# Relative-position attention between two feed-forward layers: query rows in two kinds with both halves, and head 0 staged from small transfers of the last batch

## The chip, the cores and the metric

The kernel runs on one core of a Trainium2 chip. A core has TensorE (PE, matrix products; its weight loads are listed as PEld), VectorE (DVE), ScalarE (ACT), GpSimd (POOL) and SyncE (SP), each with its own instruction stream, and 16 DMA engines that move data for all of them. Streams meet only at semaphores. The metric is the device time of one execution: before the change the median of three runs is 445.53 us (445.25 to 446.58).

## The reference

Input x is 4 batches of 512 tokens with 128 features, in float32. Three steps follow each other, each added to x:

```
x = x + 0.5 * ffn(layernorm(x))
x = x + attention(layernorm(x))          # 16 heads of width 8, with relative positions
x = x + 0.5 * ffn(layernorm(x))
ffn(x):   layernorm, product with ternary w1 (512 x 128), gelu, layernorm, product with ternary w2
attention(x):
  content = (q + u) k^T ;  pos = relative_shift((q + v) P^T),  P = sinusoids @ Wp + bp
  out = softmax((content + pos) / sqrt(8)) v ;  return out @ Wo + bo
```

The relative shift makes row s of the positional scores up to column s from query s, and the columns from s + 2 on from query s + 1.

## The kernel before, in words

The program has three stretches: the first feed-forward with the projections of attention at its end, the 16 heads, and the output projection with the second feed-forward. `ffn` is a software pipeline written out by hand: each engine's stream runs through the same steps n = 0 to 26, and `QK_STEPS` says that the query and key products of batch 0, 1, 2, 3 stand at steps 17, 20, 22, 24. The value products (`v_product`, L1066, in 16 groups) stand between and behind them.

Scores are made in float16 at float32 precision by splitting queries, keys and positions into a high and a low half. PE makes a projection, ACT writes the high halves (`q_high_halves`, L566; `k_high_half`, L574), DVE the low halves (`q_low_halves`, L854; `k_low_half`, L866, for batch 3), and POOL extends the positional query by the first 64 entries of the next position (L481, L482) and makes the low keys of batches 0 to 2 (L486). `uh, ul` are the halves of q + u, `vh, vl` those of q + v, `kh, kl` those of the key.

The products of one head need these values with other rows on the partitions than the projections leave them on. So all of them go through scratch in device memory: SP writes each batch for all 16 heads at once (the loop at L340, seven transfers of 256 KB a batch: three of queries to `qs_scratch`, two of content rows to `qc_scratch`, two of keys to `kc_scratch`), and each head is then loaded into `stage_q`, `stage_c`, `stage_k` and `stage_z`, which have two halves each (`par`), so that one head is loaded while another is computed. For head 0, POOL loads the content rows of all batches and two of the eight pieces of `stage_q`, and SP the other six (L362) and the keys (L364), once `q_out` and `k_out` say that every write has landed.

A head has 16 score tiles q of 128 rows (four column groups j of PE with 32 rows each: 4 batches by 8 positions; the query position is 128 j + 8 q + i). One tile (`scores`, L1102) is four rounds over the four column groups: the content product (L1116, 512 columns), the low query half against the high positions (L1122, 512 columns), the high query half against both position halves for the columns up to the diagonal (L1128, a0 + 8 columns, a0 = 128 j + 8 q) and the next query's high half for those behind it (L1133, 510 - a0 columns). Two tiles make a pair in a PSUM pair (three PSUM pairs take turns). For each pair DVE takes the row maxima (`row_max`, L886), ACT the exponentials (L633), DVE turns them (`turn`, L894), and PE multiplies them with the values (`values`, L1139), one head later. Heads 0, 1, 2 and 15 are written out; heads 3 to 14 are a loop of six rounds of two heads on each engine.

Before head 0 PE waits for the copies of all values, for the folded output bias (L1097 on PE, L876 on DVE, semaphore `bo_ready`) and for head 0's loads.

## Time and profile before

| | |
|---|---|
| median of three runs | 445.53 us |
| the profiled execution's own time | 447.46 us |
| its span, first to last instruction | 445.3 us |
| busy: DVE, PE, ACT, POOL | 398.2 us (89%), 357.0 us (80%), 263.9 us (59%), 113.4 us (25%) |
| DMA queues | 30.67 MB, mean 69 GB/s |

The times in the rows below count from the first instruction, so the time outside the span (447.46 - 445.3 = 2.16 us) lies around them. A busy share is an average over the three stretches. The chain of waits is followed back from the last instruction; at each step it names what released it. "issue" in a bracket is idle time of an engine for which the profile shows no wait.

### The profile page before, as it was taken

To read this page: it belongs to the slowest core of one execution; us is meant where nothing else is said; L and a number is where in the kernel's file an instruction comes from. 1 tells how busy PE (TensorE), PEld (TensorE's weight loads), DVE (VectorE), ACT (ScalarE), POOL (GpSimd) and SP (SyncE) were. 2 spreads that over 40 slices of the span, in tenths; PEclk is the share of its full clock that TensorE was granted. 3 is DMA by queue.
4 is the path that set the end of the run, shared out by engine and by line. 5 is a ranking of instruction groups with operands and counts; after the bars stand their busy time and mean duration, and the time that the engine had idled before them with its cause. 6 is when DMAs were issued, how large, how long until landed. Compare 5 with 4: busy or idle time off the path is not lost.

```text
span 445.3 us, 18049 instructions
## 1 busy us (share of the span) xinstructions
PE 357.0 (80%) x7328; PEld 288.1 (65%) x7328; DVE 398.2 (89%) x579; ACT 263.9 (59%) x650; POOL 113.4 (25%) x157
## 2 busy tenths in 40 slices
PE   1869898756979889898898987988989889676974
PEld 1647675645767767677676766776767767573664
DVE  8786988429999999999999999999999999948685
ACT  1666555316666666666666666666666666614980
POOL 7543745390020201202102022020120210025552
PEclk9988899969899999999999999999999999988898
DMA  7005147920322313213133132231321301500002
GB/s 213 1 1 186 51 148 245 296 62 12 81 57 43 81 26 87 68 31 84 40 65 75 19 88 56 44 80 20 88 64 30 89 7 25 75 18 2 0 26 71
DMA packets 60182, 30.67 MB, mean 69 GB/s; under 512 B 36880, under 2 KB 58928, under 8 KB 60016
## 3 DMA queue, kind: packets, MB, share of 16 engines
q1 hardware_dynamic: 59376, 29.22, 25.8%
q10 hardware_dynamic: 576, 0.73, 0.6%
q8 instruction: 27, 0.44, 0.4%
q0 software_dynamic: 192, 0.18, 0.2%
q14 instruction: 11, 0.09, 0.1%
HBM read 19.11 MB, written 11.01 MB: 68 GB/s over the span
## 4 chain that ended last, share of the span: by engine, by line
DVE 58%; issue 17%; PE 11%; ACT 5%; POOL 2%; SPq 2%; DMA 2%; DVEq 1%; POOLq 0%; ACTq 0%
DVE pT L894 30%; DVE negmax L886 19%; PE pair L1014 3%; ACT v_rep L602 2%; DVE xh L702 2%; ACT v_rep L590 1%; PE pair L969 1%; DVE v_rep L820 1%; DVE sqsum L814 1%; DMA qs_scratch<-pT 1%; SPq L309 1%; PE pair L1183 1%; DMA stage_k<-kc_scratch 1%; DVE stat L692 1%; PE pair L1116 1%
## 5 line engine op out<-in xcount | busy, mean ns | idle before, releaser
L633 ACT ACTIVATE probs<-pair,negmax 128x512 f32<-128x512 f32 x256 | 173.7, 683 | 111.3 <-DVE negmax L886 111.3
L886 DVE TENSOR_REDUCE negmax<-pair 128x2 f32<-128x1024 f32 x128 | 152.1, 1188 | 10.4 <-PE pair L1133 10.4
L894 DVE STREAM_TRANSPOSE pT<-probs 128x1024 f32<-128x1024 f32 x128 | 157.0, 1226 | 0.5 <-ACT probs L633 0.5
L1116 PE MATMUL pair<-stage_k,stage_c 128*32 128x512 f16 x1024 | 117.2, 408 | 47.4 <-ACT probs L633 40.8
L1122 PE MATMUL pair<-stage_z,stage_q 128*32 128x512 f16 x1024 | 111.4, 384 | 0.0
L1133 PE MATMUL pair<-stage_z,stage_q 128*32 128x438 f16 (+58 forms) x1024 | 102.9, 282 | 0.0
L508 POOL COPY v_diag<-v_rep 32x512 f32 (+1 forms) x64 | 38.9, 607 | 233.9 <-PE pair L1148 226.5
L1128 PE MATMUL pair<-stage_z,stage_q 128*32 128x16 f16 (+50 forms) x1024 | 97.9, 277 | 0.0
L1148 PE MATMUL pair<-pT,v_diag 128*32 128x128 f32 (+1 forms) x2176 | 93.3, 271 | 3.6 <-DVE pT L894 3.6
L1116 PEld LDWEIGHTS pair<-stage_k,stage_c 128*32 128x32 f16 x1024 | 50.7, 140 | 69.5 <-ACT probs L633 55.4
L1148 PEld LDWEIGHTS pair<-pT,v_diag 128*32 128x32 f32 x2176 | 73.3, 114 | 4.1 <-DVE pT L894 3.8
L1133 PEld LDWEIGHTS pair<-stage_z,stage_q 128*32 128x32 f16 x1024 | 47.8, 136 | 11.9 <-issue 1.2
L1128 PEld LDWEIGHTS pair<-stage_z,stage_q 128*32 128x32 f16 x1024 | 47.7, 135 | 11.9 <-issue 1.6
L1122 PEld LDWEIGHTS pair<-stage_z,stage_q 128*32 128x32 f16 x1024 | 50.2, 147 | 0.0
L633 ACT ACTIVATION_READ_ACCUMULATOR probs<-pair,negmax (+1 forms) x256 | 50.1, 196 | 0.0
L1014 PEld LDWEIGHTS pair<-w2c,v_rep 128*128 128x128 f32 x256 | 35.7, 211 | 3.6 <-issue 1.5
L1014 PE MATMUL pair<-w2c,v_rep 128*128 128x129 f32 x256 | 36.9, 297 | 0.0
L590 ACT ACTIVATE v_rep<-pair,vectors,cols 128x512 f32<-128x512 f32 x32 | 25.0, 780 | 11.7 <-PE pair L1014 7.2
L602 ACT ACTIVATE v_rep<-v_rep,cols 128x512 f32<-128x512 f32 x32 | 23.2, 725 | 1.2 <-DVE sqsum L814 1.2
L814 DVE TENSOR_TENSOR sqsum<-sqsum,v_rep 128x512 f32<-128x512 f32 x16 | 14.2, 884 | 6.3 <-ACT v_rep L602 5.5
L702 DVE TENSOR_SCALAR xh<-x,mv,rs 128x128 f32<-128x128 f32 x48 | 16.7, 410 | 3.2 <-POOL rs L440 3.2
L969 PE MATMUL pair<-ident,xh 128*128 128x128 f32 x48 | 12.8, 357 | 7.5 <-DVE xh L702 7.5
(112 smaller groups left out, 326.0 us busy)
## 6 DMA issues: line engine op xcount, KB each, us to landing
stage_z<-z_scratch SPq DMA_DIRECT2D x16, 254.0 KB
qs_scratch<-pT SPq DMA_DIRECT2D x12, 256.0 KB, 2.7
stage_q<-qs_scratch SPq DMA_DIRECT2D x126, 24.0 KB
stage_z<-z_scratch SPq DMA_DIRECT2D x16, 128.0 KB
qc_scratch<-pT SPq DMA_DIRECT2D x8, 256.0 KB, 3.5
kc_scratch<-pT SPq DMA_DIRECT2D x8, 256.0 KB, 3.5
stage_k<-kc_scratch SPq DMA_DIRECT2D x16, 128.0 KB
stage_z<-z_scratch SPq DMA_DIRECT2D x16, 127.5 KB
```

The source lines that it names most:

```text
L508: nc.gpsimd.tensor_copy(v_diag[q, par, :, quad, :], v_rep[q, :, bass.ds(h * HP, HP)]).then_inc(v_diag_ready, 1)
L590: nc.scalar.activation(ge[:, n % 8, :], ps[n % 2], ACT.Gelu, scale=wstep[:, 0:1], bias=b1c[:, c:c + 1]).then_inc(s["gelu"], 1)
L602: nc.scalar.activation(sq[:, m % 3, :], ge[:, m % 8, :], ACT.Square, bias=minus_pivot).then_inc(s["squared"], 1)
L633: nc.scalar.activation(probs[:, q % 6, :], score_pair(q // 2)[:, q % 2, :], ACT.Exp, bias=negmax[:, q % 8:q % 8 + 1], accum_out=rowsum[:, ...
L886: nc.vector.tensor_reduce(negmax[:, 2 * n % 8:2 * n % 8 + 2], score_pair(n)[:, :, :], AX.X, ALU.max, negate=True).then_inc(max_ready, 1)
L894: nc.vector.transpose(pT[:, par, 2 * n:2 * n + 2, :].rearrange("p a s -> p (a s)"), probs[:, 2 * n % 6:2 * n % 6 + 2, :].rearrange("p a s ...
L1014: ins = mm(out_tile(t), ge[:, (4 * g + c) % 8, k], w2c[:, c, :], start=(c == 0), stop=(c == HC - 1))
L1116: mm(bank[32 * j:32 * j + 32, :], all_rows[:, 32 * j:32 * j + 32], stage_k[:, par, :], start=True, stop=False, skip_group_check=True)
L1122: mm(o, rows(stage_q[:, par, 0, :], j), stage_z[:, par, 0, m0:m0 + S], start=False, stop=False, skip_group_check=True)
L1128: mm(bank[32 * j:32 * j + 32, 0:n], rows(stage_q[:, par, 1, :], j), stage_z[:, par, 1, m0:m0 + n], start=False, stop=False, skip_group_che ...
L1133: ins = mm(bank[32 * j:32 * j + 32, a0 + 2:S], rows(stage_q[:, par, 2, :], j), stage_z[:, par, 2, m0 + a0 + 2:m0 + S], start=False, stop=True,
L1148: ins = mm(ps[4 + par][32 * b:32 * b + 32, NI * q0:NI * q1], v_diag[:, par, b * KB + kb, :, :].rearrange("p j e -> p (j e)"), mov, start=( ...
```

## The change

Positional queries have two kinds instead of three: one for this position and one for the next, each with the low and the high half as rows. The positions have a low and a high version of either part. One tile is five rounds over the column groups: the content product, and then, for each position half, a0 + 8 columns with this query and 510 - a0 columns with the next. The queries of a batch are one write of 288 KB instead of three of 256 KB, and a piece of `stage_q` is 64 runs of 256 bytes instead of 192 of 128. The scratch for content and keys is laid out by head.

Head 0's keys come straight from on-chip memory (`first_keys`): POOL sends those of batches 0 to 2 behind their low halves, SP those of batch 3. The writes of batch 3 are split: what head 0 needs (the queries of its 8 features in both kinds come from 16 partitions, content from 8) goes out first; SP then sends four query pieces and the last content rows of head 0, waits until all eleven loads of its own have landed, and only then writes the keys of batch 2 and everything else of batch 3. POOL loads the other four query pieces of head 0, and, between the two spreads of the values, the eight of head 1. The halves move to another part of `pT`, and DVE's wait for all writes goes from before head 0 to the first turn of head 1; one of DVE's clears of `stage_q` at the start goes, and POOL's one.

```diff
@@ -50,18 +50,22 @@
-LOADS_FIRST = 6
-LOADS = 16
+LOADS_EVEN = 11
+LOADS_ODD = 9
+LOADS_POOL = 13
+EARLY = 2 * HP
+LOADS = 17
+ZR = ZW - ZB0
...
-    qs_dram = nc.dram_tensor("qs_scratch", (D, 2, 3, B * S), F16, kind="Internal").ap()
-    qc_dram = nc.dram_tensor("qc_scratch", (D, 4, B * S), F16, kind="Internal").ap()
-    kc_dram = nc.dram_tensor("kc_scratch", (D, 4, B, S), F16, kind="Internal").ap()
-    z_dram = nc.dram_tensor("z_scratch", (D, 2, 3, 2 * S), F16, kind="Internal").ap()
+    qs_dram = nc.dram_tensor("qs_scratch", (D, 2, B, VW), F16, kind="Internal").ap()
+    qc_dram = nc.dram_tensor("qc_scratch", (H, B, 2, HP, 2, S), F16, kind="Internal").ap()
+    kc_dram = nc.dram_tensor("kc_scratch", (H, B, 2, HP, 2, S), F16, kind="Internal").ap()
+    z_dram = nc.dram_tensor("z_scratch", (D, 2, 4, 2 * S), F16, kind="Internal").ap()
...
-        stage_q = sb("stage_q", [128, 2, 3, B * S], F16)
+        stage_q = sb("stage_q", [128, 2, B * NI, 2, NG], F16)
...
-        stage_z = sb("stage_z", [128, 2, 3, ZW], F16)
+        stage_z = sb("stage_z", [128, 2, 2, S + ZR], F16)
...
+        def first_keys(eng, b, done):
+
+            c = slice(b * S, (b + 1) * S)
+            for a in range(2):
+                r = 32 * b + 16 * a
+                eng.dma_start(stage_k[r:r + 16, 0, :], rep_ap(half[0:HP, 2 + a, c], [(0, 2), (1, S)]))\
+                    .then_inc(done, 16)
 
         def stage_queries(eng, h, par, done, rows_i=range(NI)):
-            q_rows = qs_dram.rearrange("(h p) t k n -> h (p t) k n", p=HP)[h]
+            q_rows = qs_dram.rearrange("(h p) t b n -> h (p t) b n", p=HP)[h]
             for ii in rows_i:
                 i = NI - 1 - ii
-                src = q_rows.rearrange("r k (b m) -> r (k b) m", b=B)[:, :, i * NG:(i + 1) * NG]
-                dst = stage_q[16 * ii:16 * ii + 16, par, :, :].rearrange(
-                    "r k (b m) -> r (k b) m", b=B)[:, :, i * NG:(i + 1) * NG]
-                eng.dma_start(dst, src).then_inc(done, 16)
+                dst = stage_q[16 * ii:16 * ii + 16, par, :, :, :].rearrange("r (b i) k g -> r b i (k g)", b=B)[:, :, i]
+                eng.dma_start(dst, q_rows[:, :, i * NG:(i + 2) * NG]).then_inc(done, 16)
+
+        def write_queries(eng, b, r, done):
+
+            eng.dma_start(qs_dram[r, :, b, :], rep_ap(vl[r, b, :], [(VQ, 2), (1, VW)])).then_inc(done, 16)
+
+        def write_content(eng, b, h0, h1, done):
+            c = slice(b * S, (b + 1) * S)
+            for a in range(2):
+                eng.dma_start(qc_dram[h0:h1, b, a].rearrange("h p d n -> h (p d n)"), half[HP * h0:HP * h1, 0:2, c])\
+                    .then_inc(done, 16)
+
+        def write_keys(eng, b):
+            c = slice(b * S, (b + 1) * S)
+            for a in range(2):
+                eng.dma_start(kc_dram[:, b, a].rearrange("h p d n -> h (p d n)"),
+                              rep_ap(half[:, 2 + a, c], [(0, 2), (1, S)])).then_inc(k_out, 16)
...
-            for b in range(B):
-                c = slice(b * S, (b + 1) * S)
-
-                sp.wait_ge(q_split, 2 * b + 1)
-                sp.dma_start(qs_dram[:, :, 1, c], rep_ap(vh[:, b, :], [(0, 2), (1, S)])).then_inc(q_out, 16)
+            for b in range(B - 1):
+
                 sp.wait_ge(v_extended, 2 * b + 2)
-                sp.dma_start(qs_dram[:, :, 0, c], rep_ap(vl[:, b, :], [(NG, 2), (1, S)])).then_inc(q_out, 16)
-                sp.dma_start(qs_dram[:, :, 2, c], rep_ap(vh[:, b, NG:], [(0, 2), (1, S)])).then_inc(q_out, 16)
-
+                write_queries(sp, b, slice(0, D), q_out)
                 sp.wait_ge(q_split, 2 * b + 2)
-                for t, src in ((0, uh), (2, ul)):
-                    sp.dma_start(qc_dram[:, t:t + 2, c], rep_ap(src[:, c], [(0, 2), (1, S)]))\
-                        .then_inc(u_out[b], 16)
-                if b < B - 1:
+                write_content(sp, b, 0, H, u_out[b])
+                if b < B - 2:
                     sp.wait_ge(k_split, b + 1)
-                else:
-                    sp.wait_ge(k_split_last, 1)
-                for t in (0, 2):
-                    sp.dma_start(kc_dram[:, t:t + 2, b, :], rep_ap(kh[:, c], [(B * S, 2), (1, S)]))\
-                        .then_inc(k_out, 16)
-            sp.wait_ge(q_out, 16 * 3 * B)
-            sp.wait_ge(stage_zero, 8)
-            stage_queries(sp, 0, 0, staged[0], range(NI - 2))
-            sp.wait_ge(k_out, 32 * B)
-            stage_keys(sp, 0, 0, staged[0])
+                    write_keys(sp, b)
+            sp.wait_ge(v_extended, 2 * B)
+            write_queries(sp, B - 1, slice(0, EARLY), q_first)
+            sp.wait_ge(q_split, 2 * B)
+            write_content(sp, B - 1, 0, 1, u_first)
+            sp.wait_ge(k_split_last, 1)
+            first_keys(sp, B - 1, staged[0])
+            sp.wait_ge(q_out, 16 * (B - 1))
+            sp.wait_ge(q_first, 16)
+            sp.wait_ge(stage_zero, 6)
+            stage_queries(sp, 0, 0, staged[0], range(4))
+            sp.wait_ge(u_first, 32)
+            stage_content(sp, 0, 0, B - 1, staged[0])
+
+            sp.wait_ge(staged[0], 16 * LOADS_EVEN)
+            sp.wait_ge(k_split, B - 1)
+            write_keys(sp, B - 2)
+            write_queries(sp, B - 1, slice(EARLY, D), q_out)
+            write_content(sp, B - 1, 1, H, u_out[B - 1])
+            write_keys(sp, B - 1)
 
             for b in range(B):
                 sp.wait_ge(u_out[b], 32)
                 stage_content(sp, 1, 1, b, staged[1])
+            sp.wait_ge(k_out, 32 * B)
             stage_keys(sp, 1, 1, staged[1])
-            stage_queries(sp, 1, 1, staged[1])
...
-            nc.gpsimd.memset(stage_q[:, 1, 2, :].bitcast(U32), 0).then_inc(stage_zero, 1)
...
+                        if b < B - 1:
+                            pool.wait_ge(k_split, b + 1)
+                            first_keys(pool, b, staged_pool)
...
+                        stage_content(pool, 0, 0, b, staged_pool)
...
-            pool.wait_ge(q_out, 16 * 3 * B)
-            pool.wait_ge(stage_zero, 8)
-            stage_queries(pool, 0, 0, staged_first, range(NI - 2, NI))
-            pool.wait_ge(u_out[B - 1], 32)
-            stage_content(pool, 0, 0, B - 1, staged_first)
+            pool.wait_ge(stage_zero, 6)
+            pool.wait_ge(q_out, 16 * (B - 1))
+            pool.wait_ge(q_first, 16)
+            stage_queries(pool, 0, 0, staged_pool, range(4, NI))
...
             spread_v(0, 0)
+            pool.wait_ge(q_out, 16 * B)
+            stage_queries(pool, 1, 1, staged_second)
             spread_v(1, 1)
...
+                    act.wait_ge(z_out, 16 * 2)
...
-            for par, n in ((0, 0), (0, 1), (0, 2), (1, 0), (1, 1)):
-                nc.vector.memset(stage_q[:, par, n, :].bitcast(U32), 0).then_inc(stage_zero, 1)
+            for par in range(2):
+                for b in (0, 2):
+                    nc.vector.memset(stage_q[:, par, b * NI:(b + 2) * NI, :, :].bitcast(U32), 0)\
+                        .then_inc(stage_zero, 1)
...
-            for b in range(B):
-                dve.wait_ge(u_out[b], 32)
-            dve.wait_ge(k_out, 32 * B)
-            dve.wait_ge(q_out, 16 * 3 * B)
...
+                if n == 0 and isinstance(h, int) and h == 1:
+
+                    for b in range(B):
+                        dve.wait_ge(u_out[b], 32)
+                    dve.wait_ge(k_out, 32 * B)
+                    dve.wait_ge(q_out, 16 * B)
...
-                for j in range(4):
-                    a0 = 128 * j + NI * q
-                    o = bank[32 * j:32 * j + 32, :]
-                    m0 = S - NI - a0
-                    mm(o, rows(stage_q[:, par, 0, :], j), stage_z[:, par, 0, m0:m0 + S], start=False,
-                       stop=False, skip_group_check=True)
-                for j in range(4):
-                    a0 = 128 * j + NI * q
-                    n = a0 + NI
-                    m0 = S - NI - a0
-                    mm(bank[32 * j:32 * j + 32, 0:n], rows(stage_q[:, par, 1, :], j),
-                       stage_z[:, par, 1, m0:m0 + n], start=False, stop=False, skip_group_check=True)
-                for j in range(4):
-                    a0 = 128 * j + NI * q
-                    m0 = S - NI - a0
-                    ins = mm(bank[32 * j:32 * j + 32, a0 + 2:S], rows(stage_q[:, par, 2, :], j),
-                             stage_z[:, par, 2, m0 + a0 + 2:m0 + S], start=False, stop=True,
-                             skip_group_check=True)
+
+                for low in range(2):
+                    for j in range(4):
+                        a0 = 128 * j + NI * q
+                        n = a0 + NI
+                        m0 = S - NI - a0
+                        mm(bank[32 * j:32 * j + 32, 0:n], stage_q[:, par, :, 0, j * NQ + q],
+                           stage_z[:, par, low, m0:m0 + n], start=False, stop=False, skip_group_check=True)
+                    for j in range(4):
+                        a0 = 128 * j + NI * q
+                        n = S - a0 - 2
+                        ins = mm(bank[32 * j:32 * j + 32, a0 + 2:S], stage_q[:, par, :, 1, j * NQ + q],
+                                 stage_z[:, par, low, S:S + n], start=False, stop=low == 1, skip_group_check=True)
...
-            pe.wait_ge(staged_first, 16 * LOADS_FIRST)
-            head(0, 0, 16 * (LOADS - LOADS_FIRST), True)
-            head(1, 1, 16 * LOADS)
-            head(2, 0, 16 * (2 * LOADS - LOADS_FIRST))
+            pe.wait_ge(staged_pool, 16 * LOADS_POOL)
+            head(0, 0, 16 * LOADS_EVEN, True)
+            pe.wait_ge(staged_second, 16 * NI)
+            head(1, 1, 16 * LOADS_ODD)
```

The order on SP, from the end of batch 2 to the loads of head 1. Before, batch 2 and 3 are written whole, then head 0's queries and keys are loaded, then head 1:

```order
L344 DMA qs_scratch<-pT 256x1x512
L346 DMA qs_scratch<-pT 256x1x512
L347 DMA qs_scratch<-pT 256x1x512
L351 DMA qc_scratch<-pT 128x2x512 x2
L358 DMA kc_scratch<-pT 128x2x512 x2
L309 DMA stage_q<-qs_scratch 16x12x64 x6
L300 DMA stage_k<-kc_scratch 128x1x512
L296 DMA stage_c<-qc_scratch 32x4x128 x4
L300 DMA stage_k<-kc_scratch 128x1x512
L309 DMA stage_q<-qs_scratch 16x12x64 x8
```

On SP now, from the queries of batch 2:

```order
L325 DMA qs_scratch<-pT 256x1x576
L330 DMA qc_scratch<-pT 16x16x512 x2
L325 DMA qs_scratch<-pT 32x1x576
L330 DMA qc_scratch<-pT 16x1x512 x2
L313 DMA stage_k<-pT 16x1x512 x2
L321 DMA stage_q<-qs_scratch 16x4x128 x4
L303 DMA stage_c<-qc_scratch 32x4x128
L336 DMA kc_scratch<-pT 16x16x512 x2
L325 DMA qs_scratch<-pT 224x1x576
L330 DMA qc_scratch<-pT 15x16x512 x2
L336 DMA kc_scratch<-pT 16x16x512 x2
L303 DMA stage_c<-qc_scratch 32x4x128 x4
```

Between the end of the projections and head 0's last load, five small transfers stand on SP where seven of 256 KB stood, and the large ones stand behind head 0's loads.

The order on POOL, from the keys of batch 2 to the values' spread (`stage_c` are content rows, `v_diag` the values in the layout of the product). Before:

```order
L486 TENSOR_TENSOR pT<-pT 128x512
L296 DMA stage_c<-qc_scratch 32x4x128
L481 COPY pT<-pT 128x64
L482 COPY pT<-pT 128x64
L296 DMA stage_c<-qc_scratch 32x4x128
L309 DMA stage_q<-qs_scratch 16x12x64 x2
L296 DMA stage_c<-qc_scratch 32x4x128
L511 MEMSET v_diag 128x2048
L508 COPY v_diag<-v_rep 32x64x8 x8
```

On POOL now:

```order
L517 TENSOR_TENSOR pT<-pT 128x512
L313 DMA stage_k<-pT 16x1x512 x2
L303 DMA stage_c<-qc_scratch 32x4x128
L512 COPY pT<-pT 128x64
L513 COPY pT<-pT 128x64
L303 DMA stage_c<-qc_scratch 32x4x128
L321 DMA stage_q<-qs_scratch 16x4x128 x4
L544 MEMSET v_diag 128x2048
L541 COPY v_diag<-v_rep 32x64x8 x4
L321 DMA stage_q<-qs_scratch 16x4x128 x8
L541 COPY v_diag<-v_rep 32x64x8 x4
```

Two key transfers stand ahead of batch 3's extension, and head 1's queries are POOL's, between the two spreads.

The order on PE in the first tile of head 0. Before, four rounds of four (the two rounds of 512 columns are each one row):

```order
L1116 MATMUL pair<-stage_k,stage_c 32x512 x4
L1122 MATMUL pair<-stage_z,stage_q 32x512 x4
L1128 MATMUL pair<-stage_z,stage_q 32x8
L1128 MATMUL pair<-stage_z,stage_q 32x136
L1128 MATMUL pair<-stage_z,stage_q 32x264
L1128 MATMUL pair<-stage_z,stage_q 32x392
L1133 MATMUL pair<-stage_z,stage_q 32x510
L1133 MATMUL pair<-stage_z,stage_q 32x382
L1133 MATMUL pair<-stage_z,stage_q 32x254
L1133 MATMUL pair<-stage_z,stage_q 32x126
```

On PE now, the same tile up to the second half's first four products; the other four follow as in the first half:

```order
L1150 MATMUL pair<-stage_k,stage_c 32x512 x4
L1158 MATMUL pair<-stage_z,stage_q 32x8
L1158 MATMUL pair<-stage_z,stage_q 32x136
L1158 MATMUL pair<-stage_z,stage_q 32x264
L1158 MATMUL pair<-stage_z,stage_q 32x392
L1163 MATMUL pair<-stage_z,stage_q 32x510
L1163 MATMUL pair<-stage_z,stage_q 32x382
L1163 MATMUL pair<-stage_z,stage_q 32x254
L1163 MATMUL pair<-stage_z,stage_q 32x126
L1158 MATMUL pair<-stage_z,stage_q 32x8
L1158 MATMUL pair<-stage_z,stage_q 32x136
L1158 MATMUL pair<-stage_z,stage_q 32x264
```

A tile has 20 products instead of 16, and a column group streams 512 + 2 x 518 = 1548 columns instead of 2 x 512 + 518 = 1542.

## Rows read from the trace of the kernel before

**Rows 1.** Chain of waits, projections to head 0: start us, us, what.

```profile
73.93 0.76 DVE pT L862
...
81.22 4.43 DMA qs_scratch<-pT
...
89.84 3.66 DMA stage_k<-kc_scratch
...
93.64 0.65 PE pair L1116 x4
...
98.77 1.23 DVE negmax L886
```

**Rows 2.** Timeline, 76 to 97.5 us: start, us, engine, what, [idle before <-releaser].

```profile
77.71 0.24 POOL L482 COPY pT<-pT 128x64 f16<-128x64 f16 x1
78.43 0.74 DVE L869 SCALAR_TENSOR_TENSOR pT<-pair,vectors,pT 128x512 f16<-128x512 f32 x1
...
85.67 4.13 SPq L309 DMA_DIRECT2D stage_q<-qs_scratch  x6
...
86.78 0.55 POOL L309 DMA_DIRECT2D stage_q<-qs_scratch  x1 [0.29 <-issue]
87.28 0.28 DVE L876 TENSOR_TENSOR rows<-rows,pair 128x128 f32<-128x128 f32 x1
...
89.78 5.28 POOL L508 COPY v_diag<-v_rep 32x512 f32<-32x512 f32 x8
...
96.61 1.23 DVE L886 TENSOR_REDUCE negmax<-pair 128x2 f32<-128x1024 f32 x1 [9.05 <-PE pair L1133]
```

**Rows 3.** Busy time by stretch: us, engines' busy (instructions), granted clock, DMA share, GB/s.

```profile
79.40:83.20 3.80, 3.70 (x128) 3.49 (x128) 1.75 (x3) 1.07 (x2) 0.55 (x1) 1.00 1.03 341
83.20:84.30 1.10, 0.01 (x1) 0.00 (x2) 0.00 (x0) 0.12 (x1) 0.00 (x0) 1.00 0.82 254
...
93.60:97.80 4.20, 4.16 (x52) 2.66 (x56) 1.19 (x1) 0.00 (x0) 4.00 (x6) 0.50 0.31 66
```

**Rows 4.** Issue to landing of the `qs_scratch` transfers, 68 to 100 us.

```profile
DMA to landing us min/median/max: 2.4/2.7/4.4
```

**Rows 5.** Issue to landing of the 64 KB `attn_scratch` transfers.

```profile
DMA to landing us min/median/max: 2.0/2.1/3.8
```

**Rows 6.** Timeline of PE, 108.5 to 119 us: head 1's first product.

```profile
112.25 0.66 PE L1116 MATMUL pair<-stage_k,stage_c 128*32 128x512 f16 x4 [3.02 <-ACT probs L633]
```

**Rows 7.** Timeline, start of the program.

```profile
4.63 0.95 POOL L427 MEMSET stage_q<- 128x1024 uint32 x1
...
5.32 0.91 DVE L718 MEMSET stage_q<- 128x1024 uint32 x1 [0.16 <-issue]
...
6.14 0.81 DVE L692 BATCH_NORM_STATS2 stat<-x 128x6 f32<-128x128 f32 x4
```

**Rows 8.** Issue to landing of the transfers of x (0.7 to 2.3 us).

```profile
DMA to landing us min/median/max: 4.7/6.4/7.8
```

**Rows 9.** Timeline, one tile in the loop of heads.

```profile
174.89 0.40 PE L1122 MATMUL pair<-stage_z,stage_q 128*32 128x512 f16 x4
...
175.10 0.37 PE L1128 MATMUL pair<-stage_z,stage_q 128*32 128x208 f16 x4
...
175.32 0.42 PE L1148 MATMUL pair<-pT,v_diag 128*32 128x128 f32 x8
```

**Rows 10.** Busy time of one head in the loop.

```profile
148.95:167.01 18.06, 15.54 (x388) 12.70 (x392) 18.06 (x17) 11.74 (x34) 2.42 (x5) 1.00 0.28 63
```

**Rows 11.** Timeline, 184.5 to 189 us: the loop's jump back.

```profile
185.03 0.44 PE L1116 MATMUL pair<-stage_k,stage_c 128*32 128x512 f16 x4 [1.18 <-ACT probs L633]
...
187.40 1.19 DVE L886 TENSOR_REDUCE negmax<-pair 128x2 f32<-128x1024 f32 x1
```

**Rows 12.** The page's DMA queues: packets, MB, share of 16 engines.

```profile
q8 instruction: 27, 0.44, 0.4%
```

**Rows 13.** DMA queues from 200 to 260 us.

```profile
DMA packets 9510, 3.74 MB, mean 62 GB/s; under 512 B 7206, under 2 KB 9510, under 8 KB 9510
...
q1 hardware_dynamic: 9510, 3.74, 26.5%
```

More of the change, by code:

```diff
@@ L117, in macaron_kernel @@
         pf = pTf[:, 3584:4096]
-        half = pTf[:, 4096:8192].bitcast(F16).rearrange("p (a n) -> p a n", a=4)
+        half = pTf[:, 10240:14336].bitcast(F16).rearrange("p (a n) -> p a n", a=4)
         uh, ul, kh, kl = (half[:, n, :] for n in range(4))
+        VQ = 2 * (14336 - 8192)
         vl = pTf[:, 8192:8192 + B * VW // 2].bitcast(F16).rearrange("p (b n) -> p b n", b=B)
@@ L206, in macaron_kernel @@
         staged = [sem("staged_even"), sem("staged_odd")]
-        staged_first = sem("staged_first")
+        q_first = sem("q_first")
+        u_first = sem("u_first")
+        staged_pool = sem("staged_pool")
+        staged_second = sem("staged_second")
         v_diag_ready = sem("v_diag_ready")
@@ L325, in _ @@
             sp.wait_ge(pos_split, 2)
-            for t, kind, src in ((0, 0, 0), (1, 0, 2), (0, 1, 0), (1, 1, 1), (0, 2, 2), (1, 2, 3)):
-                sp.dma_start(z_dram[:, t, kind, :], zs[:, src, :]).then_inc(z_out, 16)
+            for t in range(2):
+                sp.dma_start(z_dram[:, t, :, :], zs).then_inc(z_out, 16)
             def stage_pos(h, par):
                 z_rows = z_dram.rearrange("(h p) t k n -> h (p t) k n", p=HP)[h]
-                for kind, lo, hi in ((0, 0, ZW), (1, 0, S), (2, ZB0, ZW)):
-                    zr = z_rows[:, kind, :]
-                    src = bass.AP(zr.tensor, zr.offset + lo, [[1, NI]] + [list(zr.ap[0])] + [[1, hi - lo]])
-                    sp.dma_start(stage_z[:, par, kind, lo:hi], src).then_inc(staged[par], 16)
@@ L336, in _ @@
[L336 removed]
+                for low in range(2):
+                    for kind, lo, at, n in ((low, 0, 0, S), (2 + low, ZB0, S, ZR)):
+                        zr = z_rows[:, kind, :]
+                        src = bass.AP(zr.tensor, zr.offset + lo, [[1, NI]] + [list(zr.ap[0])] + [[1, n]])
+                        sp.dma_start(stage_z[:, par, low, at:at + n], src).then_inc(staged[par], 16)
+            sp.wait_ge(z_out, 16 * 2)
             stage_pos(0, 0)
             stage_pos(1, 1)
[L340 to L344 removed]
+            for b in range(B - 1):
@@ L1107, in scores @@
                 bank = score_pair(q // 2)[:, q % 2, :]
-                def rows(a, j):
-                    return a.rearrange("k (b g) -> k b g", g=NG)[:, :, j * NQ + q]
                 all_rows = stage_c[:, par, :].rearrange("k (m g) -> k m g", g=NQ)[:, :, q]
@@ L1164, in head @@
                         values(h - 1, 1 - par, kb)
-            pe.wait_ge(staged_first, 16 * LOADS_FIRST)
-            head(0, 0, 16 * (LOADS - LOADS_FIRST), True)
-            head(1, 1, 16 * LOADS)
-            head(2, 0, 16 * (2 * LOADS - LOADS_FIRST))
+            pe.wait_ge(staged_pool, 16 * LOADS_POOL)
+            head(0, 0, 16 * LOADS_EVEN, True)
+            pe.wait_ge(staged_second, 16 * NI)
+            head(1, 1, 16 * LOADS_ODD)
+            head(2, 0, 16 * (LOADS + LOADS_EVEN))
             with pe.Fori(0, (H - 4) // 2) as it:
                 for k in range(2):
-                    head(it * 2 + (3 + k), 1 - k, (it + (2 + k)) * (16 * LOADS) - 16 * LOADS_FIRST * k)
-            head(H - 1, 1, (H // 2) * 16 * LOADS)
+                    head(it * 2 + (3 + k), 1 - k,
+                         (it + (1 + k)) * (16 * LOADS) + 16 * (LOADS_EVEN if k else LOADS_ODD))
+            head(H - 1, 1, 16 * ((H // 2 - 1) * LOADS + LOADS_ODD))
             for kb in range(KB):
```

11 lines of the change are left out of this document (4 added, 7 removed).

## The prediction

> **What bounds the kernel now.** Start with the busy time of one head in the loop: in 18.06 us DVE is busy for all 18.06 and PE for 15.54 [rows 10]. From its second row maximum on, DVE sets the pace of the heads, and PE waits for banks. So an edit of the products is worth something only where PE runs out of those 2.5 us, and an edit of the transfers only where DVE waits. Next read the chain of waits: between the projections (DVE, 73.93) and the second row maximum of head 0 (98.77) it runs over a landing of `qs_scratch`, a landing of `stage_k`, and PE at 93.64 [rows 1]. The timeline says the same from DVE's side: its first row maximum starts at 96.61 after 9.05 us idle, though the last projection half was made at 78.43 + 0.74 = 79.17 [rows 2]. In between, the DMA share is 1.0 at 341 GB/s [rows 3]: SP's large writes fill the DMA engines, and the loads of head 0 stand behind them. When PE gets its data it is at half clock (0.50 of full, 1.2 GHz) after the idle time [rows 3]. This stretch is what the change edits.
>
> **The change part by part.**
>
> *Head 0's loads.* All of this is worked out from rows of one execution, which took 447.46 us; the savings are taken off the median, 445.53, which is 1.93 below it.
> The last extension ends at 77.71 + 0.24 = 77.95 [rows 2]. Ahead of it POOL now issues two key transfers, 0.55 each as its other issues [rows 2]; part of that 1.1 falls into a wait for DVE, and I take 78.6 (77.95 to 79.05). SP was still issuing for batch 2 then; now it has three transfers in that batch instead of seven and is free. It issues five small transfers and then four query pieces and a content row. Its pitch in the loads of before is 4.13 / 6 = 0.69 [rows 2], so the loads begin at 78.6 + 5 x 0.69 = 82.05 and the fifth is issued at 84.8. The first transfer's landing (2.1 by the 64 KB transfers, 3.8 at most [rows 5]) is at 80.7 to 82.4, hidden behind the issues up to 3.45. The last load lands 2.7 later (2.4 to 4.4, [rows 4]): 87.5, bounds 87.2 to 89.2. POOL's four pieces start after that first landing and its content row at about 81.3; with 0.55 + 0.29 a piece [rows 2] the last is issued at 83.8 and lands at 86.5.
> What would be late next is the bias on DVE, 87.28 + 0.28 = 87.56 [rows 2], at the end of the value products. These lose 1.10 us between 83.20 and 84.30, with PE and PEld idle, right behind a stretch of exactly 128 products (256 instructions with their weight loads) at DMA share 1.03 [rows 3]. I read that as PE waiting for its next block of instructions behind the writes, since 27 transfers of 0.44 MB in all are 16 KB each [rows 12]. With fewer writes the stall may go, and then this gate is at 86.5. So PE starts head 0 at 87.6 (86.5 to 89.4) instead of 93.64.
>
> *The clock.* PE is then idle for about 1 us between the value products and head 0. After 1.18 us idle it took 0.44 for a 512-column product [rows 11], after the long wait 0.65 [rows 1]; I take full clock. A tile's last three rounds take 0.43 [rows 9] and the first, of 512 columns like the second, 0.22: 0.65 in all. Two pairs are 2.6 us, so the second row maximum, the step at which DVE's pace sets in, starts at 87.6 + 2.6 + 0.1 = 90.3 instead of 98.77: 8.5 saved. Bounds: with PE at 86.5 9.6 saved; with PE at 89.4 and at half clock, 98.77 - 93.64 = 5.13 for the two pairs as before [rows 1], 94.5, 4.3 saved.
>
> *The held-back writes.* They are 512 + 252 + 480 + 512 = 1756 KB, at 341 GB/s [rows 3] 5.3 us, begun at 87.5 and landed by 95 with 2.1 for the last. Behind them SP issues head 1's content rows and keys: seven writes and five loads at 0.69 end at 95.8, landed by 100.2 at the slow bound. On POOL the first four copies of the values (half of 5.28 [rows 2]) end near 91; the queries have landed near 92 (third of SP's writes); eight pieces at 0.84 are issued until 97.8 and landed at 100.5 (102.2 at 4.4). The spread of head 1's values waits behind them, but it is used a head later. Head 1 started 112.25 - 98.77 = 13.5 after the second row maximum [rows 1, 6], released by a bank and not by its loads; that is 103.8 now. So the writes are hidden with 1.6 to 3.6 us to spare. They do load the DMA engines while PE fetches head 0's products: one stall as at 83.20, up to 1.10. PE is one pair ahead of DVE then, so I take 0.3 (0 to 1.1).
>
> *The start.* DVE's clears are 0.91 with 0.16 between [rows 7]; one less lets its first statistics start 1.07 earlier, at 5.07, but x needs 0.7 + 4.7 = 5.4 to land [rows 7, 8]. POOL loses 0.95 [rows 7]. So up to 0.7 is gained at the head of a chain that continues into the feed-forward; part goes into PE's slow start. I take 0.4 (0 to 0.7).
>
> *The products.* In the loop, round 2 starts at 174.89, round 3 at 175.10 and the next work behind round 4 at 175.32 [rows 9]: rounds 3 and 4 together cost 0.22, as round 2 does (0.21), since the short and the long columns add up to 518 in each column group. Replacing round 2 by another round 3 and 4 costs 0.01 a tile, 0.2 a head. Were each added round of four to cost a further 0.1, it would be 1.6 a head, still inside PE's 2.5. DVE hides it: 0. Positions, layout of the scratch and the longer runs of `stage_q` are loads one head ahead: 0.
>
> Sum: -8.5 - 0.4 + 0.3 = -8.6, so 445.53 - 8.6 = 436.9.
>
> **The rivals.**
>
> *Late loads.* Two transfers in a row at their slow bounds (3.8 and 4.4), or SP's issue of odd shapes slower than 0.69. For it: the chain has two landings in series, and issues have taken longer while the engines were full. Against: the writes ahead are small and the engines nearly empty by then. PE starts at 89.4, cold, and DVE at 94.5: -4.3 - 0.4 + 0.3, 441.1. If POOL's issues slow down beside DVE, head 1 is late by a few us instead; same price.
>
> *The loop of heads outgrows PE's instruction store.* This is the one on the other side. A head in the loop has 256 + 128 = 384 products (x388 counted [rows 10]) and as many weight loads; two heads are 1536 instructions, 6 blocks of 256. From 200 to 260 us all 9510 packets are those of the data queue [rows 13], so before the change PE jumps back five times without fetching anything. Now two heads are 2 x 448 x 2 = 1792 instructions, 7 blocks. If they no longer fit, with edges and the block fetched ahead, each jump waits for a block. Under full DMA engines a block took 3.8 + 1.1 = 4.9 us [rows 3]; a small transfer lands in 2.1 [rows 5]. Hidden at the jump are 1.18 of idle PE and the 187.40 - (185.03 + 1.6) = 0.8 by which the first pair is early [rows 11], 2.0 in all. Five jumps cost 5 x 0.1 = 0.5 to 5 x 2.9 = 14.5. It outweighs the gain when a block takes over 2.0 + 8.6 / 5 = 3.7 us; at 4.9 the time is 451.4. Half way, at 3.3, it is 443.4. For it: 7 is more than any loop in this trace. Against: the fetches may be short at the DMA share of 0.28 in the loop [rows 10].
> The Trainium skill, in "Runtime: NRT & Kernel Launch" under "Instruction fetch mechanics", gives PE 128 KiB of instruction memory, 2048 instructions in 16 KiB blocks, and says that a taken branch whose target is not in the current two-page window must fetch the target before going on. The trace disagrees on the window: a loop of 6 blocks was not fetched again [rows 13]; with 8 blocks in all, 7 blocks that start inside one, and one ahead, would be 9, and the sum would be the rival's.
>
> *The stretch is bound by something else.* If the value products and the bias keep their place and clock, PE cannot start before 87.6 anyway; that is in the forecast. No row speaks for a gate later than that.
>
> **How the numbers follow.** The forecast, 436.9, has a chance of 0.56, with its own range 435 to 439.5. Late loads (or a late head 1): 0.22. The loop fetching again: 0.20, of which 0.07 below 441, 0.05 between 441 and 446.9, 0.08 beyond. Others 0.02. The range 434.8 to 443 leaves out some 0.15. A difference of under 0.3%, 1.3 us, cannot be told from none: faster means below 444.2, slower above 446.9. From the cases: faster 0.85, same 0.06, slower 0.09.
>
> **What would show it.** Right: no 1.1 us hole in the value products; PE's first product of head 0 near 87.6 at clock 1.0; the second row maximum near 90; head 1's first product released by ACT; a head of 18.06 us in the loop with PE busy about 15.8; instruction transfers of the page up from 27 to about 30 only (six written heads or loop bodies by 128 more instructions are 3 blocks), none inside the loop. Wrong: DVE idle in the loop right behind a jump, with instruction packets there; PE released by `stage_q` or `stage_c` after 89; head 1 released by a landing; DVE busy under 18.0 of each 18.06.

## The result, and the profile after

The kernel after takes 454.17 us (median of four runs, 451.56 to 457.29) against 445.43 for the kernel before beside it (445.25 to 446.58): a ratio of 1.018, 95% interval 1.014 to 1.022. It is slower by 8.7 us; the forecast was 436.9 with a range to 443.0. The profiled execution took 454.7 us, with a span of 452.6 (before: 447.46 and 445.3).

Head 0 starts as early as forecast, and earlier. The chain of waits of the kernel after, from the projections to the first row maximum (start us, us, what), answers to [rows 1]:

```profile
70.49 0.76 DVE pT L900
...
78.98 0.65 SPq L321
...
81.60 2.83 DMA stage_c<-qc_scratch
...
84.56 0.41 PE pair L1150 x2
...
86.33 1.24 DVE negmax L919
```

The timeline of the same stretch (start, us, engine, what, [idle before <-releaser]) answers to [rows 2]:

```profile
74.95 0.24 POOL L513 COPY pT<-pT 128x64 f16<-128x64 f16 x1
...
76.66 3.70 PE L1122 MATMUL pair<-pT,xT 128*32 128x128 f32 x128 [0.79 <-issue]
...
80.67 2.34 PE L1122 MATMUL pair<-pT,xT 128*32 128x128 f32 x74 [0.31 <-issue]
...
83.66 0.28 DVE L914 TENSOR_TENSOR rows<-rows,pair 128x128 f32<-128x128 f32 x1
...
84.56 0.44 PE L1150 MATMUL pair<-stage_k,stage_c 128*32 128x512 f16 x4 [1.13 <-DMA stage_c<-qc_scratch]
...
87.81 1.23 DVE L919 TENSOR_REDUCE negmax<-pair 128x2 f32<-128x1024 f32 x1 [0.26 <-PE pair L1163]
```

The second row maximum, from which DVE sets the pace, starts at 87.81 instead of 98.77 [rows 1]: 10.96 us earlier. 3.44 of that came before the change's stretch (the chain's first row at 70.49 instead of 73.93), 7.5 in it. The busy time by stretch (us, PE, PEld, DVE, ACT, POOL busy with their instructions, granted clock with 1.00 for TensorE's full speed, DMA share, GB/s) has the projections' end without the full DMA engines of [rows 3], head 0's first products at full clock, a head in the loop, and the first 4 us behind one of the loop's jumps:

```profile
75.00:84.00 9.00, 7.33 (x235) 6.46 (x226) 4.29 (x8) 3.60 (x5) 4.62 (x9) 1.00 0.35 80
84.50:88.00 3.50, 3.44 (x99) 3.37 (x102) 1.42 (x2) 0.41 (x1) 1.89 (x4) 1.00 0.65 179
...
148.95:167.01 18.06, 16.07 (x452) 14.05 (x448) 18.06 (x17) 11.66 (x34) 2.43 (x4) 1.00 0.23 56
...
176.00:180.00 4.00, 3.13 (x48) 2.52 (x52) 0.83 (x2) 1.09 (x4) 0.32 (x1) 0.57 0.36 96
```

So a head still takes 18.06 us with DVE busy throughout, as in [rows 10]; PE's part rose from 15.54 to 16.07. The last row shows where the time went: DVE busy for 0.83 of 4 us. All five jumps look like that in the timeline. PE's first product of a round and DVE's first row maximum of it stand below, and last PE's first product behind the loop, where nothing jumps back; [rows 11] has the same place of before:

```profile
173.39 0.69 ACT L669 ACTIVATE probs<-pair,negmax 128x512 f32<-128x512 f32 x1 [0.81 <-DVE negmax L919]
...
176.87 0.66 PE L1150 MATMUL pair<-stage_k,stage_c 128*32 128x512 f16 x4 [3.72 <-ACT probs L669]
...
179.83 1.22 DVE L919 TENSOR_REDUCE negmax<-pair 128x2 f32<-128x1024 f32 x1 [3.17 <-PE pair L1163]
...
216.09 0.44 PE L1150 MATMUL pair<-stage_k,stage_c 128*32 128x512 f16 x4 [3.54 <-ACT probs L669]
217.88 1.23 DVE L919 TENSOR_REDUCE negmax<-pair 128x2 f32<-128x1024 f32 x1 [1.81 <-PE pair L1163]
...
255.13 0.66 PE L1150 MATMUL pair<-stage_k,stage_c 128*32 128x512 f16 x4 [4.54 <-ACT probs L669]
258.09 1.23 DVE L919 TENSOR_REDUCE negmax<-pair 128x2 f32<-128x1024 f32 x1 [3.98 <-PE pair L1163]
...
295.12 0.44 PE L1150 MATMUL pair<-stage_k,stage_c 128*32 128x512 f16 x4 [4.31 <-ACT probs L669]
297.39 1.22 DVE L919 TENSOR_REDUCE negmax<-pair 128x2 f32<-128x1024 f32 x1 [3.07 <-PE pair L1163]
...
334.23 0.66 PE L1150 MATMUL pair<-stage_k,stage_c 128*32 128x512 f16 x4 [3.93 <-ACT probs L669]
337.19 1.23 DVE L919 TENSOR_REDUCE negmax<-pair 128x2 f32<-128x1024 f32 x1 [3.36 <-PE pair L1163]
...
371.07 0.44 PE L1150 MATMUL pair<-stage_k,stage_c 128*32 128x512 f16 x4 [1.16 <-ACT probs L669]
```

The brackets name ACT, because its exponential was the last semaphore that PE needed. It is not the cause: the exponential that frees the first bank ended at 173.39 + 0.69 = 174.08, and PE started 2.8 us later. Before, PE began 1.18 us after its last work [rows 11]; behind the loop it still does (1.16). What PE waited for shows in the times of the instruction transfers: in each round the first one behind the jump starts 1.3 to 2.7 us after the jump, and PE's first weight load comes 2.7 to 3.2 us after that start. Three of the five restarts are at half clock (0.66 for a 512-column product instead of 0.44); a fourth, at 295.12, begins at full clock and falls to half within its first pair (0.52 from 296.0 to 298.0 us).

DVE's waits in the heads, 110 to 385 us (line waited for: us in total, times, longest):

```profile
DVE negmax L919 <- PE pair L1163: 15.4, 5, 4.0
```

The page's DMA queues (packets, MB, share of 16 engines) have more instruction transfers than [rows 12]; at 1.23 MB for 75 they too are 16 KB each:

```profile
q8 instruction: 75, 1.23, 1.2%
```

and the queues from 200 to 260 us, where [rows 13] had none, now show them inside the loop:

```profile
q1 hardware_dynamic: 6800, 3.19, 20.6%
q8 instruction: 14, 0.23, 1.7%
```

The account, profiled run against profiled run: second row maximum -10.96; from there to the last turn 391.94 - 87.81 = 304.13 instead of 386.56 - 98.77 = 287.79, +16.34, of which the five waits are 15.4; behind it +1.92. Together +7.3, the difference of the spans. Of the 1.92, 1.63 stand at the tail's 32 turns on PE (L1214), which took 5.47 us here and 3.84 before; in the written-out kernel below they take 3.84 again.

### The profile page after: what moved, and what is told of

The parts are those of the page before. It is cut to its first block, busy times and chain, and to the rows that moved or that the text cites. A ratio compares the mean times of both kernels' runs of the same rounds, so it can differ in the third digit from the quotient of the medians.

```text
span 452.6 us, 20122 instructions
## 1 busy us (share of the span) xinstructions
PE 367.0 (81%) x8352; PEld 313.5 (69%) x8352; DVE 398.4 (88%) x578; ACT 263.8 (58%) x650; POOL 120.3 (27%) x171
## 3 DMA queue, kind: packets, MB, share of 16 engines
q8 instruction: 75, 1.23, 1.2%
## 4 chain that ended last, share of the span: by engine, by line
DVE 57%; issue 17%; PE 12%; ACT 7%; POOL 3%; SPq 1%; DVEq 1%; DMA 1%; POOLq 0%; ACTq 0%
DVE pT L933 29%; DVE negmax L919 19%; PE pair L1053 3%; ACT v_rep L638 2%; PE pair L1163 2%; PE pair L1150 2%; DVE xh L738 2%; ACT v_rep L626 1%; PE pair L1008 1%; PE pair L1214 1%; ACT probs L669 1%; DVE v_rep L858 1%; DVE sqsum L852 1%; PE pair L1158 1%; ACT xT L598 1%
## 5 line engine op out<-in xcount | busy, mean ns | idle before, releaser
L1163 PE MATMUL pair<-stage_z,stage_q 128*32 128x510 f16 (+34 forms) x2048 | 181.7, 287 | 0.0
L1158 PE MATMUL pair<-stage_z,stage_q 128*32 128x8 f16 (+34 forms) x2048 | 170.5, 283 | 0.0
L1150 PE MATMUL pair<-stage_k,stage_c 128*32 128x512 f16 x1024 | 134.5, 409 | 44.3 <-ACT probs L669 40.5
L919 DVE TENSOR_REDUCE negmax<-pair 128x2 f32<-128x1024 f32 x128 | 152.2, 1189 | 18.6 <-PE pair L1163 18.5
L1158 PEld LDWEIGHTS pair<-stage_z,stage_q 128*32 128x32 f16 x2048 | 135.6, 142 | 0.4
L1163 PEld LDWEIGHTS pair<-stage_z,stage_q 128*32 128x32 f16 x2048 | 112.8, 138 | 11.1 <-issue 2.3
L1177 PE MATMUL pair<-pT,v_diag 128*32 128x128 f32 (+1 forms) x2176 | 103.4, 268 | 3.5 <-DVE pT L933 3.5
L1150 PEld LDWEIGHTS pair<-stage_k,stage_c 128*32 128x32 f16 x1024 | 60.9, 142 | 62.6 <-ACT probs L669 55.3
L1053 PEld LDWEIGHTS pair<-w2c,v_rep 128*128 128x128 f32 x256 | 34.6, 205 | 3.5 <-issue 1.4
L1053 PE MATMUL pair<-w2c,v_rep 128*128 128x129 f32 x256 | 35.7, 291 | 0.0
L1008 PEld LDWEIGHTS pair<-ident,xh 128*128 128x128 f32 x48 | 7.4, 160 | 13.9 <-DVE xh L738 10.9
L1122 PE MATMUL pair<-pT,xT 128*32 128x128 f32 x512 | 15.4, 274 | 1.8 <-issue 1.1
```

The source lines that it names most:

```text
L919: nc.vector.tensor_reduce(negmax[:, 2 * n % 8:2 * n % 8 + 2], score_pair(n)[:, :, :], AX.X, ALU.max, negate=True).then_inc(max_ready, 1)
L1053: ins = mm(out_tile(t), ge[:, (4 * g + c) % 8, k], w2c[:, c, :], start=(c == 0), stop=(c == HC - 1))
L1150: mm(bank[32 * j:32 * j + 32, :], all_rows[:, 32 * j:32 * j + 32], stage_k[:, par, :], start=True, stop=False, skip_group_check=True)
L1158: mm(bank[32 * j:32 * j + 32, 0:n], stage_q[:, par, :, 0, j * NQ + q], stage_z[:, par, low, m0:m0 + n], start=False, stop=False, skip_grou ...
L1163: ins = mm(bank[32 * j:32 * j + 32, a0 + 2:S], stage_q[:, par, :, 1, j * NQ + q], stage_z[:, par, low, S:S + n], start=False, stop=low == ...
L1177: ins = mm(ps[4 + par][32 * b:32 * b + 32, NI * q0:NI * q1], v_diag[:, par, b * KB + kb, :, :].rearrange("p j e -> p (j e)"), mov, start=( ...
```

## The experiments

Two theories went in. *The store*: PE's loop body, 1818 instructions with its waits and branch instead of 1562, no longer stays in PE's instruction memory, so each jump waits for it to be fetched. *The work*: five rounds of products instead of four use up PE's spare time at the place where the heads change, and PE comes late by itself.

**The loop written out on PE alone**, in the kernel after (no jump is left; same products):

```diff
-            with pe.Fori(0, (H - 4) // 2) as it:
+            for it in range((H - 4) // 2):
                 for k in range(2):
                     head(it * 2 + (3 + k), 1 - k,
```

> The changed kernel with PE's loop over heads 3 to 14 written out, so that PE never jumps back; nothing else differs. Theory S (store): a loop of two heads of 896 instructions no longer stays in PE's instruction store, and each of five jumps waits for a block; DVE's five waits of together 15.4 us in the changed kernel go, and the time falls from 454.2 to about 439 (437 to 441), with instruction fetches spread evenly over the heads. Theory W (work): PE is late at a head's end because of 64 more products and weight loads a head; the time stays within 451 to 457.

Measured: 437.39 us (436.80 to 438.97) against 446.01 for before in that batch; ratio 0.979 (0.973 to 0.985). DVE's waits from 110 to 385 us are gone but for one of another kind:

```profile
DVE pT L933 <- ACT probs L669: 0.5, 1, 0.5
```

The page counts 65 instruction transfers here too, since straight code has to be fetched once as a whole:

```profile
q8 instruction: 65, 1.06, 1.0%
```

So neither the work nor the number of transfers costs time in the heads; what costs is waiting for them behind a jump. This kernel beats both others.

**The same edit in the kernel before.**

> The kernel before with PE's loop written out. Theory S: its loop of 6 blocks was kept, so its five jumps cost nothing and writing it out gives nothing: 445.4, within 1.3 us. If jumps cost something whatever the size of the loop, it gets faster by what five jumps cost (over 3 us).

Measured: 446.06 (445.26 to 447.25) against 446.01, ratio 0.998 (0.995 to 1.001). Before the change the jumps cost nothing, so the gain above is not one that writing out gives by itself.

**The kernel before with a body as long as after's.** Four products of one column more in each tile, which write where the content product then writes:

```diff
                 bank = score_pair(q // 2)[:, q % 2, :]
 
+                for j in range(4):
+                    mm(bank[32 * j:32 * j + 32, 0:1], stage_c[:, par, 0:32], stage_k[:, par, 0:1],
+                       start=True, stop=True, skip_group_check=True)
```

> The kernel before with four one-column products ahead of each tile (their result is overwritten by the tile's first round). PE's program is then as long as the changed one's, instruction for instruction in number (1818 from loop start to jump, at the same place), but transfers, queries and columns are those of before. Theory S: the five stalls come back, 445.4 + 15.4 = 461 (455 to 464), with some 75 instruction transfers on the page instead of 27. Theory W: four products of one column cost at most 0.1 us a tile, which PE's 2.5 idle us a head hide: 445 to 447.

Measured: 464.55 (463.27 to 467.65) against 446.01, ratio 1.040 (1.032 to 1.048). The page and DVE's waits (110 to 390 us):

```profile
q8 instruction: 75, 1.23, 1.1%
```

```profile
DVE negmax L886 <- PE pair L1136: 18.4, 9, 4.6
```

That is 0.55 above the range expected. The 18.5 us that it lost are about these 18.4 (before has one such wait, of 0.4). Five of the nine waits stand behind the five jumps (2.1 to 4.6 each), the others are under 0.6. Nothing of the change is in this kernel but the length.

**The kernel after with a loop of three rounds of four heads**, two jumps instead of five:

```diff
-            with pe.Fori(0, (H - 4) // 2) as it:
-                for k in range(2):
+            with pe.Fori(0, (H - 4) // 4) as it:
+                for k in range(4):
...
```

> The changed kernel with four heads in PE's loop and three rounds instead of two heads and six rounds: two jumps instead of five. Theory S: three stalls fewer, 454.2 - 3 x 3.1 = 445 (442 to 448). Theory W: no change, 451 to 457.

Measured: 445.01 (444.01 to 447.60) against 446.01, ratio 0.998 (0.994 to 1.001). DVE's waits, two of them behind jumps (3.9 each):

```profile
DVE negmax L919 <- PE pair L1163: 8.1, 3, 3.9
```

Five, two and no jumps give 454.2, 445.0 and 437.4: 3.4 to 3.8 us a jump. Each of the two jumps is followed by 16 instruction transfers, for a body of 3634 instructions, where the five have 9 each, and costs about the same: PE waits for the code at the jump, and the rest comes while it works. The store holds; the work falls.

**The written-out kernel again, as the base of the next two.**

> The kernel after with the loop of heads written out on PE, again, as the base of the next three runs. It should repeat 437.4 (436.8 to 439.0).

Measured: 438.88 (438.59 to 439.39) against 446.13, ratio 0.983 (0.978 to 0.988). It repeats within 1.5 us. The trace shows a difference at head 0: PE's first product takes 0.44 here too, but then the clock falls (0.55 from 86.5 to 90.3 us), and the second row maximum starts at 90.37 instead of 88.04 in the first run.

**The clears of before at the start**: the fifth on DVE and POOL's ahead of its first layer norm.

```diff
+            nc.gpsimd.memset(stage_q[:, 1, 2 * NI:4 * NI, :, :].bitcast(U32), 0).then_inc(stage_zero, 1)
             nc.gpsimd.memset(v_diag[:, 0, :, :, :], 0.0).then_inc(v_diag_zero, 1)
...
-            for par in range(2):
-                for b in (0, 2):
-                    nc.vector.memset(stage_q[:, par, b * NI:(b + 2) * NI, :, :].bitcast(U32), 0)\
-                        .then_inc(stage_zero, 1)
+            for n in (0, 2):
+                nc.vector.memset(probs[:, n:n + 2, :].bitcast(U32), 0)
+            for par, b in ((0, 0), (0, 2), (1, 0)):
+                nc.vector.memset(stage_q[:, par, b * NI:(b + 2) * NI, :, :].bitcast(U32), 0).then_inc(stage_zero, 1)
```

> The kernel after with PE's heads written out, and at the start the number of clears of before: five on DVE and one of POOL's ahead of its first layer norm (two of DVE's five clear a buffer that nothing reads until it is rewritten). If the fewer clears are worth what DVE's first normalised tile shows, 8.76 to 7.87 or 8.33, this run takes 0.4 to 0.9 more than its base: 437.8 to 438.3, and the first row maximum of head 0 moves by as much. Rival: the earlier start changes the clock or the overlap inside the first feed-forward and so is worth the whole 3.4 by which its last step came earlier in the profiled run; then this run takes 440.5 to 441.

Measured: 439.56 (438.37 to 439.73), 0.7 above its base, with ranges that overlap. So the start is not worth 3.4; what it is worth is not settled. In the two profiled runs the clears make DVE's first normalised tile 0.62 us later (8.76 for 8.14), but the last step of the projections only 0.07 (75.70 for 75.63). The first row maximum moved by 1.61 (89.40 for 87.79), more than expected, and that came behind the projections: SP's first small write is issued 0.39 later and PE's first product is at half clock (0.65).

**Without holding back**: SP sends the 1756 KB right ahead of head 0's pieces.

```diff
             first_keys(sp, B - 1, staged[0])
+            sp.wait_ge(k_split, B - 1)
+            write_keys(sp, B - 2)
             sp.wait_ge(q_out, 16 * (B - 1))
+            write_queries(sp, B - 1, slice(EARLY, D), q_out)
+            write_content(sp, B - 1, 1, H, u_out[B - 1])
+            write_keys(sp, B - 1)
             sp.wait_ge(q_first, 16)
...
-            sp.wait_ge(staged[0], 16 * LOADS_EVEN)
-            sp.wait_ge(k_split, B - 1)
-            write_keys(sp, B - 2)
-            write_queries(sp, B - 1, slice(EARLY, D), q_out)
-            write_content(sp, B - 1, 1, H, u_out[B - 1])
-            write_keys(sp, B - 1)
```

> The kernel after with PE's heads written out, where SP sends the keys of batch 2 and the large writes of batch 3 (1756 KB) right ahead of head 0's four query pieces and content row, instead of behind their landing; head 0's small writes and its keys from on-chip memory stay as they are. If holding back is what makes head 0 early, the writes cost their own time in the DMA engines, 1756 KB at 341 GB/s = 5.1 us, and seven issues at 0.7 us on SP ahead of the loads, 4.9 us: the first row maximum goes from 86.5 to some 91.5 and the time to 442.5 (441 to 444). Rival: the small writes and direct keys alone give the gain, since the loads share the engines with the writes: SP's issues still cost some, and the time is 437.5 to 439.5.

Measured: 444.65 (443.61 to 447.42) against 438.88 for the base: 5.8 lost, a little more than expected, and the first row maximum is at 93.56 instead of some 91.5. The timeline shows how:

```profile
79.71 1.28 SPq L336 DMA_DIRECT2D kc_scratch<-pT  x2
...
85.42 2.81 SPq L321 DMA_DIRECT2D stage_q<-qs_scratch  x4
...
90.63 0.65 PE L1149 MATMUL pair<-stage_k,stage_c 128*32 128x512 f16 x4 [8.55 <-DMA stage_c<-qc_scratch]
...
93.56 1.23 DVE L918 TENSOR_REDUCE negmax<-pair 128x2 f32<-128x1024 f32 x1 [10.98 <-PE pair L1162]
```

SP issues the writes for 85.42 - 79.71 = 5.7 us before it comes to the loads, and PE then starts at half clock. With the writes sent first, the rest of the change gives 446.13 - 444.65 = 1.5 us.

**Where the store ends.** The padding of above with two and with three products a tile, in bodies of 1690 and 1754 instructions:

> The kernel before with two more products of one column in every score tile (they write where the content product then writes, so the result is the same): PE's loop of heads has 1690 instructions, between the 1562 of before, which were not fetched again, and the 1818 of after, which were. If what counts is the whole of some 2048 instructions with a block of 256 fetched ahead, the loop touches 8 blocks and is fetched again each round: 65 to 75 instruction transfers, DVE waits of 3 to 4 us behind each of five jumps, 457 to 463. Rival: a loop below 7 blocks (1792) stays: 27 to 30 transfers, no such waits, 446 to 447 (two short products a tile are 0.1 us each at most, inside PE's spare time).

Measured: 445.98 (444.67 to 446.32) against 446.13, ratio 0.998 (0.995 to 1.001), and on the page

```profile
q8 instruction: 29, 0.48, 0.4%
```

That is the second expectation; the first fails. The body of 1690 stays, with no instruction transfer between its jumps, and two short products a tile cost nothing.

> The kernel before with three more products of one column in every score tile: PE's loop has 1754 instructions. 1690 were kept and 1818 fetched again. If seven whole blocks of 256 (1792) can be kept, this one stays: 27 to 30 instruction transfers, no waits behind the jumps, 446 to 447. Rival: the block fetched ahead and the loop's unaligned ends count too and the limit lies between 1690 and 1754: 65 to 75 transfers, DVE waits of 3 to 4 us at five jumps, 457 to 463.

Measured: 469.23 (467.94 to 470.52) against 448.18 for before in that batch, ratio 1.048 (1.034 to 1.062); page and DVE's waits (110 to 390 us):

```profile
q8 instruction: 75, 1.23, 1.1%
```

```profile
DVE negmax L886 <- PE pair L1136: 23.7, 9, 5.3
```

64 instructions more a body turn a kernel as fast as before into one that is 21 us slower, more than the rival expected: the five waits behind the jumps are 3.5 to 5.3. The limit lies between 1690 and 1754 here. The padding also moves the body's start (by 96 instructions from the one to the other), so whether its length or its place against the blocks decides is open. The traces speak for the place: in the first round 6 instruction transfers start while the body of 1690 runs, as with the 1562 of before, and 7 with 1754, as with 1818. So the bodies that stay seem to touch 7 blocks and the others 8. No run moves a body without lengthening it.

## Why the prediction was wrong

**The step that failed** is "The products": "DVE hides it: 0", which priced the 256 added instructions by PE's time alone. By PE's time it was right: a head takes 18.06 as before, PE 16.07 of it (forecast about 15.8), and the written-out kernel takes 287.98 us from the second row maximum to the last turn (376.02 - 88.04), before 287.79. The cost is in the jumps, and with these the term is +15.4, DVE's five waits, instead of 0. That is more than the 8.6 to be gained.

**The rival that came true** was on record, with "The loop of heads outgrows PE's instruction store" at a chance of 0.20, and 0.08 for slower than 446.9. Three parts of it, against the runs:

- Whether it happens. The argument against, "the fetches may be short at the DMA share of 0.28", was no reason: with a share of 0.23 over a head and 0.42 to 0.47 in the waits themselves PE still waits 3.54 to 4.54 us. Counting length in whole blocks could not decide it: 1690 and 1754 are both under 7 blocks of 256, and only the 1690 stay.
- The wait. The rival's block took 2.1 to 4.9 us and broke even at 3.7; the five waits add up to 20.04, 4.0 each. The 2.0 that hide at a jump were right: 4.0 - 2.0 makes 10.0 for five.
- The restart, which the rival left out. From PE's first product to DVE's row maximum it is 2.96, 1.79, 2.96, 2.27 and 2.96, instead of the 1.6 that the rival took for a first pair: 4.9 more for five, 4.1 of it behind the three restarts at half clock and 0.7 behind the one whose clock fell. 10.0 + 4.9 = 14.9, and the trace has 15.4. The middle estimate (a block at 3.3 us, 443.4) has 6.5 of it; the longer waits are another 3.5, and the restart the 4.9.

How much is fetched was also taken too small. Of the 75 transfers 30 were expected without any inside the loop; the other 45 are 9 blocks behind each of five jumps, counted in the trace: the whole body is fetched again, not only the block that the jump lands in. When PE starts again, only the first of the 9 has started. The Trainium skill says in "Runtime: NRT & Kernel Launch", "Instruction fetch mechanics", that this memory is a FIFO refilled in blocks of 256, and that a taken branch to a page outside its window must fetch the target first. The 9 blocks and the waits agree with that; its window of two pages doesn't (1690 instructions, six and a half blocks, stay), and of the 2048 instructions that it gives PE a loop could use less than 1754 here.

**Head 0's loads**: right, but for the last step. Counted from the last extension (74.95 + 0.24 = 75.19 instead of the 78.6 assumed), the loads begin 3.8 us later (forecast 3.45), the last is issued at 6.4 (6.2), lands 2.83 after (2.7), and PE starts at 9.4 (9.0). That landing is what PE waits for, 1.13 us; the bias, 83.94 at its end, is not. From PE's first product to the second row maximum it is then 3.25 (87.81 - 84.56) instead of 2.7. With the 0.4 by which PE starts later this leaves 7.5 of the 8.5 that the stretch was to give.

**The hole of 1.10 us in the value products**: not gone. It is smaller behind the 128 products (0.31 instead of 1.12 in PE's timeline), but PE now stands 0.79 ahead of them, where it was 0.16: 1.10 together instead of 1.28. The timeline of before has

```profile
79.47 3.70 PE L1083 MATMUL pair<-pT,xT 128*32 128x128 f32 x128 [0.16 <-issue]
...
84.29 2.34 PE L1083 MATMUL pair<-pT,xT 128*32 128x128 f32 x74 [1.12 <-issue]
```

After the change the DMA share is 0.70 in the hole of 0.79, 0.61 in that of 0.31 and 0.24 between them, so full DMA engines are not the reason, or not the only one. It cost nothing, since PE waits longer for the loads.

**The clock**: right in this trace and the first written-out one, 0.44 for the first product and 1.00 over head 0's start, but in part by luck. In the three other traces that hold the writes back (the written-out kernel again, the one with the clears, the loop of four heads) PE starts head 0 at half clock or falls to it, 0.50 to 0.55 in its first pairs, and the second row maximum starts at 90.31 to 91.17 instead of 87.81 or 88.04. What decides is open.

**The held-back writes**: they are hidden, as forecast. Behind them DVE waits 0.46 once, at head 1 (0.43 before), and sending them first costs 5.8. The +0.3 for their load on the DMA engines is not singled out by a run.

**The start**: 0.4 forecast; not resolved (0.7 in time, 0.07 at the end of the projections). The 3.44 us by which the projections' row came earlier are mostly not the change's: it stands at 71.50 in the kernel before written out and at 70.95 in the one with two more products a tile, which both have the clears of before, 2.43 and 2.98 earlier than in [rows 1].

Without the loop's jumps the sum stands in total, 437.4 and 438.9 measured, 436.9 forecast, though not each of its terms is shown.

## What to carry to other kernels

Before a loop body is made longer, count its instructions on the engine that loops, weight loads included, and look whether instruction transfers stand inside the loop in the trace; work that is free by its engine's busy time can push the body out of the instruction memory, and then every jump waits: here 3.5 to 4.5 us on PE, with the DMA engines less than half busy. Where a body is near the limit, write it out or make fewer and longer rounds: the straight code of the heads was fetched ahead without a wait. And a wait between an engine's last and first work around a jump is not that of the semaphore in its bracket when that engine was done before.

## What was not expected of the hardware

- PE kept a loop of 1690 instructions over six rounds without fetching, and fetched one of 1754 or 1818 again in each, 9 blocks of 16 KiB a jump. The shorter of the two cost more, 21 us against 18.5.
- A jump cost DVE 1.8 to 5.3 us, and the time of the wait did not tell the clock behind it: after 3.54 us idle PE came back at full clock and stayed there, after 4.31 it came back at full clock and fell to half within a pair, after 3.72, 3.93 and 4.54 it came back at half. Why is open.
